# Splitting the first dense layer into three float32r products in a recommender kernel (AutoInt)

## Chip, cores and metric

One core of one Trainium2 chip runs the whole kernel. The time is the device time of one execution in microseconds (us), as the median of several runs. TensorE is called PE below, VectorE DVE, ScalarE ACT, GpSimd POOL and the queue of SyncE SP.

## The reference

```python
offsets = jnp.arange(NUM_FIELDS, dtype=X.dtype) * VOCAB_PER_FIELD
embed_x = emb_table[X + offsets[None, :]]          # 2048 x 39 x 64
att = embed_x
for i in range(LAYERS):                            # 3
    att = _mhsa(att, WQ[i], WK[i], WV[i], WR[i])   # 2 heads, softmax over 39 fields, + x @ Wr, relu
att_output = jax.nn.relu(att.reshape(B, FLAT) @ Wlin)
h = embed_x.reshape(B, FLAT)                       # 2048 x 2496
h = jax.nn.relu(h @ W1 + b1)                       # 512 wide: the layer that changes
h = jax.nn.relu(h @ W2 + b2)                       # 256 wide
dnn_output = jax.nn.relu(h @ W3 + b3)
return jax.nn.sigmoid(att_output + dnn_output)
```

All inputs are float32.

## The kernel before

The batch of 2048 is cut into 16 tiles of 128 samples. A tile has 24 units: 3 attention layers of 8 units, each unit 16 samples. One step of the main loop handles one unit at several stages, so a tile takes 24 steps (numbered `ts` 0 to 23) and the kernel 384 steps and a few more. Every engine runs a program of its own, in the order that is written out by hand; only semaphores order the engines against each other.

In step s PE does, in this order: two split products into the banks X0 and X1 (three float32r matmuls each: low part times high weight, high part times low weight, high times high), one piece of the dense branch (`dense`), a transpose of one chunk of embeddings (`embedding`, in 20 of the 24 steps), a third split product into Ob, eight transposes of the softmax of unit s-2, the scores of unit s (32 matmul records, into the bank SV) and the attention of unit s-2 (into Ob). The scores wait until ACT has copied the values of the unit before out of SV (`v_ready`).

The dense branch of a tile is spread over its steps. The first dense layer has FC = 20 chunks of 128 rows of W1 (the last has 64) and `first_layer` does one of them in each step ts = 0 to 18 and 23: embT[chunk] as weights (128 x 128), w1[chunk] as moving operand (128 x 512), into bank Mb. Both are float32. A float32 matmul stands in the trace as two records. The steps 19 to 22 hold the transposes of h1 and the second layer.

ACT does in a step: relu of Ob into xs (layers 0 and 1), copy of the transposed embedding chunk into embT, x_hi (a rounding of xs to float32r), two copies yv, the exponential, the copy v_sb and the two copies pt. DVE does: two maxima mx, two subtractions sd, in 8 of 24 steps the weighted output `prod`, x_lo = xs - x_hi, in 8 steps the sum over `prod` (`summed`, at ts = SUM_AT onwards), and, once ACT has written the exponential, den, rd and pn. POOL issues the gathers of embedding rows and shuffles embT into xs for the next tile.

Ahead of the loop, the weights come in on SP's queue (W1 in one transfer of 4,864 KB and one of 128 KB), PE and DVE make the split attention weights (`weights_ready`), and PE, ACT and DVE transpose, copy and shuffle the first tile in NB = 5 blocks of 4 chunks. POOL may run 20 gathers ahead and goes on as blocks are transposed.

Of the kernel before, what the change touches and what calls it, by code (L numbers as in the profile page):

```python
# [14 lines left out]
def autoint(nc, X, table, WQ, WK, WV, WR, W1, b1, W2, b2, W3, b3, Wlin, out):  # L15
# [42 lines left out]
    L2_AT = H1T_AT + 1  # L58
    L2_LAST = L2_AT + len(L2_PARTS) - 1

    SUM_AT = 4
# [45 lines left out]
    with ctx:  # L107
# [13 lines left out]
        w1 = sb("w1", [128, FC, N1])  # L121
# [13 lines left out]
        xs = sb("xs", [128, L, XC])  # L135
        prod = sb("prod", [128, UL, C])
# [8 lines left out]
        pe_sb = sb("pe_sb", [KR, G, H, F])  # L145
# [31 lines left out]
        weights_ready = sem("weights_ready")  # L177
        idx_ready = sem("idx_ready")
# [42 lines left out]
        LD_D = 16 * 7  # L221
# [15 lines left out]
        def layer_of(u):  # L237
            return (u % NU) // UL
# [11 lines left out]

        def layer_cols(u):

            return slice((u % UL) * C, (u % UL + 1) * C)

        def x_pair(u, e, p):
            at = (u % UL) * C + p * F
            return xs[64 * e:64 * e + D, layer_of(u), at:at + F]
# [6 lines left out]
        def _(sp):  # L264
# [9 lines left out]
            for e in range(2):  # L274
                sp.dma_start(wl_in[:, e, :], Wlin.rearrange("(f d) o -> f (d o)", f=F)).then_inc(ld_w, 16)
            sp.dma_start(w1[:, 0:FC - 1, :],
                         W1[0:(FC - 1) * 128, :].rearrange("(c p) n -> p c n", p=128)).then_inc(ld_d, 16)
            sp.dma_start(w1[0:LASTW, FC - 1, :], W1[(FC - 1) * 128:, :]).then_inc(ld_d, 16)
# [4 lines left out]
            sp.dma_start(b3_b[:], b3[None, :].to_broadcast([128, 1])).then_inc(ld_d, 16)  # L283

# [71 lines left out]
        def _(pe):  # L356
# [111 lines left out]
            pe.wait_ge(first_embT, NB)  # L468
            first_layer(0, 0)
# [42 lines left out]
        def _(act):  # L512
# [13 lines left out]
            def split_high(u):  # L526
# [6 lines left out]
                nc.scalar.copy(x_hi[:, u % XS, :], xs[:, layer_of(u), layer_cols(u)]).then_inc(xh_ready, 1)  # L533

            act.wait_ge(weights_ready, 1)
            for k in range(NB):
                first_embedding(k)
            for u in range(LEAD):
                split_high(u)
            for s in range(STEPS):  # L540
                t, ts = tile_step(s)
                u = s - NEW_AT
                if 0 <= u < TOTAL and layer_of(u) < L - 1:
                    act.wait_ge(o_ps, u + 1)
                    nc.scalar.activation(xs[:, layer_of(u) + 1, layer_cols(u)], Ob[:, 0:C], ACTF.Relu).then_inc(x_new, 1)  # L545
# [22 lines left out]
                if 0 <= u < TOTAL:  # L568
                    at_least(act, o_ps, u)
                    for j in range(2):  # L570
                        act.wait_ge(t_ps, 2 * u + j + 1)
                        nc.scalar.copy(pt[:, j * (G // 2):(j + 1) * (G // 2), :, :].rearrange("q g b f -> q (g b) f"),  # L572
                                       XB[j][0:KR, :].rearrange("q (n f) -> q n f", f=64)[:, :, 0:F]).then_inc(pt_ready, 1)
            act.wait_ge(fin_pe, 2)
# [136 lines left out]
```

## Time and profile before

| | |
|---|---|
| median of 3 runs | 2049.63 us (2048.24 to 2055.91) |
| the profiled execution | 2049.93 us, span 2048.0 us |
| PE busy | 95% of the span |
| DVE, ACT, POOL busy | 79%, 63%, 42% |
| share of PE in the chain that ended last | 94% |
| mean granted TensorE clock | 0.994 |

The profile shows one execution. Its span is the time from the first instruction to the last; the rest of its 2049.93 us lies around it. Matmuls are pipelined, so their recorded durations overlap; how far apart their ends are tells what one costs. The chain of waits gives just that, as the time that each piece adds.

### The profile page before, as it was taken

To read this page: it belongs to the slowest core of one execution; us is meant where nothing else is said; L and a number is where in the kernel's file an instruction comes from. 1 tells how busy PE (TensorE), PEld (TensorE's weight loads), DVE (VectorE), ACT (ScalarE), POOL (GpSimd) and SP (SyncE) were. 2 spreads that over 40 slices of the span, in tenths; PEclk is the share of its full clock that TensorE was granted. 3 is DMA by queue.
4 is the path that set the end of the run, shared out by engine and by line. 5 is a ranking of instruction groups with operands and counts; after the bars stand their busy time and mean duration, and the time that the engine had idled before them with its cause. 6 is when DMAs were issued, how large, how long until landed. Compare 5 with 4: busy or idle time off the path is not lost.

```text
span 2048.0 us, 103306 instructions
## 1 busy us (share of the span) xinstructions
PE 1954.7 (95%) x44640; PEld 1612.0 (79%) x44640; DVE 1614.2 (79%) x3429; ACT 1289.5 (63%) x3269; POOL 860.0 (42%) x949
## 2 busy tenths in 40 slices
PE   1598999999999999999999999999999999999998
PEld 0377888887888888888888888888888888887887
DVE  2376778887787888878788787888888788887887
ACT  0265666666666666666666666666666666666665
POOL 6544354444444444454444434444443444443000
PEclk9999999999999999999999999999999999999999
DMA  4111111111111111111111111111111111111000
GB/s 151 23 28 25 31 27 32 29 30 31 27 33 27 31 29 30 31 29 31 29 30 29 28 33 27 32 29 30 31 27 33 27 32 28 30 30 26 21 19 17
DMA packets 67561, 64.61 MB, mean 32 GB/s; under 512 B 23768, under 2 KB 54504, under 8 KB 67112
## 3 DMA queue, kind: packets, MB, share of 16 engines
q1 hardware_dynamic: 47144, 37.52, 6.2%
q0 software_dynamic: 19968, 20.49, 5.1%
q8 instruction: 357, 5.85, 1.2%
q14 instruction: 92, 0.75, 0.1%
HBM read 27.24 MB, written 0.01 MB: 13 GB/s over the span
## 4 chain that ended last, share of the span: by engine, by line
PE 94%; another core or an unknown queue 2%; issue 1%; DVE 1%; POOL 1%; SPq 1%; ACT 0%; DMA 0%; ACTq 0%
PE SV L445 21%; PE Ob L462 14%; PE Mb L400 13%; PE X L430 13%; PE X L423 9%; PE X L425 5%; PE X L424 5%; PE Ob L423 3%; PE Ob L424 3%; PE Ob L425 3%; PE Ob L391 2%; PE Mb L416 1%; POOL emb L324 1%; PE Mb L411 0%
## 5 line engine op out<-in xcount | busy, mean ns | idle before, releaser
L324 POOL DMA_INDIRECT emb<-L_rec_emb_table,idx_t x624 | 630.1, 1010 | 792.4 <-PE Ob L462 615.1
L666 DVE TENSOR_REDUCE den<-pe_sb 103x16 f32<-103x624 f32 x384 | 308.5, 803 | 316.3 <-ACT pe_sb L561 311.5
L445 PE MATMUL SV<-yv,xs 64*39 64x142 f32 x12288 | 455.0, 286 | 11.6 <-ACT v_sb L563 10.9
L445 PEld LDWEIGHTS SV<-yv,xs 64*39 64x39 f32 x12288 | 345.2, 113 | 53.0 <-issue 14.1
L545 ACT ACTIVATE xs<-Ob 128x312 f32<-128x312 f32 x256 | 110.6, 432 | 388.2 <-PE Ob L462 388.2
L648 DVE TENSOR_REDUCE mx<-SV 103x8 f32<-103x312 f32 x768 | 332.7, 474 | 26.9 <-PE SV L445 20.4
L462 PEld LDWEIGHTS Ob<-pt,v_sb 39*32 39x32 f32 x12288 | 273.2, 106 | 92.8 <-issue 91.8
L430 PE MATMUL X<-ident,pn 103*103 103x103 f32 x3072 | 341.8, 254 | 0.0
L572 ACT COPY pt<-X 103x312 f32<-103x312 f32 x768 | 284.8, 424 | 78.6 <-PE X L430 39.1
L400 PE MATMUL Mb<-w,embT 128*128 128x512 f32 (+1 forms) x640 | 331.7, 599 | 0.9 <-ACT embT L518 0.7
L462 PE MATMUL Ob<-pt,v_sb 39*32 39x39 f32 x12288 | 324.1, 198 | 7.8 <-issue 6.6
L653 DVE TENSOR_TENSOR sd<-SV,mx 103x312 f32<-103x312 f32 x768 | 330.5, 471 | 0.1
L430 PEld LDWEIGHTS X<-ident,pn 103*103 103x103 f32 x3072 | 329.7, 170 | 0.0
L671 DVE TENSOR_TENSOR pn<-pe_sb,rd 103x624 f32<-103x624 f32 x384 | 311.7, 812 | 13.3
L555 ACT COPY yv<-X 128x312 f32<-128x312 f32 x768 | 297.7, 433 | 35.9 <-PE X L425 17.7
L462 PE MATMUL Ob<-pt,v_x 39*32 39x39 f32 x12288 | 313.1, 198 | 3.5 <-issue 2.7
L301 POOL COPY xs<-embT 64x256 f32<-64x256 f32 x300 | 222.7, 742 | 214.9 <-ACT embT L524 78.9
L561 ACT ACTIVATE pe_sb<-sd 103x624 f32<-103x624 f32 x384 | 284.3, 740 | 2.2 <-DVE sd L653 2.1
L423 PE MATMUL X<-x_lo,w_hi 128*128 128x312 f32 x768 | 276.5, 360 | 2.8 <-DVE x_lo L607 2.0
L462 PEld LDWEIGHTS Ob<-pt,v_x 39*32 39x32 f32 x12288 | 262.7, 106 | 3.9 <-issue 3.1
L425 PE MATMUL X<-x_hi,w_hi 128*128 128x312 f32 x768 | 236.1, 307 | 1.7 <-issue 1.7
L424 PE MATMUL X<-x_hi,w_lo 128*128 128x312 f32 x768 | 236.1, 307 | 1.2 <-issue 1.2
(71 smaller groups left out, 2336.6 us busy)
## 6 DMA issues: line engine op xcount, KB each, us to landing
v_x<-v_sb SPq DMA_DIRECT2D x768, 39.0 KB
emb<-L_rec_emb_table,idx_t POOLq DMA_INDIRECT x624
w<-L_rec_W SPq DMA_DIRECT2D x1, 4864.0 KB
w<-L_rec_W SPq DMA_DIRECT2D x1, 512.0 KB
idx_in<-r_X SPq DMA_DIRECT2D x1, 312.0 KB, 3.9
b_b<-L_rec_b SPq DMA_DIRECT2D x1, 256.0 KB
w<-L_rec_W SPq DMA_DIRECT2D x1, 128.0 KB
b_b<-L_rec_b SPq DMA_DIRECT2D x1, 128.0 KB
```

Of the source, the lines that this page charges most:

```text
L324: nc.gpsimd.indirect_dma_start(out=emb[:, n % ER, f % 2 * D:(f % 2 + 1) * D], out_offset=None, in_=table, in_offset=bass.IndirectOffsetOnA ...
L400: return nc.tensor.matmul(Mb[:], embT[0:w, t % 2, n, :], w1[0:w, n, :], start=(n == 0), stop=(n == FC - 1))
L423: nc.tensor.matmul(out_ps, w_hi[:, l, at:at + 128], x_lo[:, slot, :], start=True, stop=False)
L424: nc.tensor.matmul(out_ps, w_lo[:, l, at:at + 128], x_hi[:, slot, :], start=False, stop=False)
L425: return nc.tensor.matmul(out_ps, w_hi[:, l, at:at + 128], x_hi[:, slot, :], start=False, stop=True)
L430: last = nc.tensor.transpose(XB[j][0:KR, g * 128:g * 128 + KR], pn[:, u % PS, j * (G // 2) + g, :, :].rearrange("q h f -> q (h f)")[:, 0:K ...
L445: last = nc.tensor.matmul(SV[64 * b:64 * b + F, at:at + YR], x_pair(u, e, p), yv[64 * e:64 * e + D, l, p, :], start=True, stop=True, skip_ ...
L462: last = nc.tensor.matmul(Ob[po:po + DH, p * F:(p + 1) * F], v, pt[lo:lo + F, g, b, :], start=False, stop=True, skip_group_check=True)
L648: nc.vector.tensor_reduce(mx[:, regions(j), :], sv_scores[:, regions(j)], AX.X, ALU.max).then_inc(mx_ready, 1)
L653: nc.vector.tensor_tensor(sd[:, gs], sv_scores[:, gs], mx[:, gs, :, None].to_broadcast([KR, G // 2, H, F]), ALU.subtract).then_inc(sd_read ...
L666: nc.vector.tensor_reduce(den[:], pe_sb[:], AX.X, ALU.add).then_inc(den_ready, 1)
L671: nc.vector.tensor_tensor(pn[:, s % PS, :, :, 0:F], pe_sb[:], rd[:, :, :, None].to_broadcast([KR, G, H, F]), ALU.mult).then_inc(pn_ready, 1)
```

## The change

W1 is no longer kept in float32. It comes in chunk by chunk through four slots, which lie in the second buffer of xs; ACT rounds each chunk into w1_hi and DVE writes the remainder w1_lo, both float32r. In the loop ACT rounds a chunk of embT into c_hi at the end of a step (`convert_high`), and DVE writes c_lo = embT - c_hi right behind x_lo (`convert_low`), for the chunk that PE uses two steps later. PE then does three float32r matmuls of 512 columns in place of one float32 matmul. To make room, the inputs of layers 1 and 2 share one buffer of xs, the weighted outputs go there too, and the exponential is written over sd. `summed` begins at ts = 0 and no longer at ts = 4.

```diff
+    CONVERT_AHEAD = 2
+    CR = 3
+    WS = 4
-    SUM_AT = 4
+    SUM_AT = 0
...
-        w1 = sb("w1", [128, FC, N1])
+        w1_hi = sb("w1_hi", [128, FC, N1], F32R)
+        w1_lo = sb("w1_lo", [128, FC, N1], F32R)
...
-        xs = sb("xs", [128, L, XC])
-        prod = sb("prod", [128, UL, C])
+        c_hi = sb("c_hi", [128, CR, TB], F32R)
+        c_lo = sb("c_lo", [128, CR, TB], F32R)
+        xs = sb("xs", [128, 2, XC])
+        w1_in = xs[:, 1, 0:WS * N1].rearrange("q (s n) -> q s n", n=N1)
...
-        pe_sb = sb("pe_sb", [KR, G, H, F])
+        pe_sb = sd
...
+        def converted_at(s):
+            t, n = tile_step(s + CONVERT_AHEAD + 1)
+            return (t, n) if n < FC and t < TILES else None
...
+            for n in range(FC):
+                w = LASTW if n == FC - 1 else 128
+                at_least(sp, w1_lo_ready, n - WS + 1)
+                sp.dma_start(w1_in[0:w, n % WS, :], W1[n * 128:n * 128 + w, :]).then_inc(ld_w1[n % WS], 16)
...
             def first_layer(t, n):
-                w = LASTW if n == FC - 1 else 128
-                if t > 0:
-                    pe.wait_ge(embT_ready, chunk_count(t, n))
+                i = t * FC + n
+                pe.wait_ge(c_lo_ready, i + 1)
                 if n == 0:
                     at_least(pe, h2_ready, t)
-                return nc.tensor.matmul(Mb[:], embT[0:w, t % 2, n, :], w1[0:w, n, :], start=(n == 0), stop=(n == FC - 1))
+                nc.tensor.matmul(Mb[:], c_lo[:, i % CR, :], w1_hi[:, n, :], start=(n == 0), stop=False)
+                nc.tensor.matmul(Mb[:], c_hi[:, i % CR, :], w1_lo[:, n, :], start=False, stop=False)
+                return nc.tensor.matmul(Mb[:], c_hi[:, i % CR, :], w1_hi[:, n, :], start=False, stop=(n == FC - 1))
...
+            pe.wait_ge(w1_lo_ready, FC)
             first_layer(0, 0)
...
+            def convert_high(t, n):
+                i = t * FC + n
+                w = LASTW if n == FC - 1 else 128
+                chunk_embedded(act, t, n)
+                if i >= CR:
+                    at_least(act, o_ps, (i - CR) // FC * NU + (i - CR) % FC - PV_AT)
+                    act.wait_ge(c_lo_ready, i - CR + 1)
+                nc.scalar.copy(c_hi[0:w, i % CR, :], embT[0:w, t % 2, n, :]).then_inc(c_hi_ready, 1)
...
             for k in range(NB):
+                for n in range(k * BK, (k + 1) * BK):
+                    w = LASTW if n == FC - 1 else 128
+                    act.wait_ge(ld_w1[n % WS], 16 * (n // WS + 1))
+                    nc.scalar.copy(w1_hi[0:w, n, :], w1_in[0:w, n % WS, :]).then_inc(w1_hi_ready, 1)
                 first_embedding(k)
...
+                    if layer_of(u) == 0:
+                        at_least(act, lin_sum, (u // NU - 1) * UL + u % UL + 1)
...
+            def convert_low(t, n):
+                i = t * FC + n
+                w = LASTW if n == FC - 1 else 128
+                dve.wait_ge(c_hi_ready, i + 1)
+                nc.vector.tensor_tensor(c_lo[0:w, i % CR, :], embT[0:w, t % 2, n, :], c_hi[0:w, i % CR, :],
+                                        ALU.subtract).then_inc(c_lo_ready, 1)
```

On ACT, a step of the loop of the second tile, with an output of layer 0 or 1 and an embedding chunk, reads before:

```order
L533 CAST x_hi<-xs 128x312 [waits o_ps,x_new]
L555 COPY yv<-X 128x8x39 [waits y_ps,sv_ps]
L555 COPY yv<-X 128x8x39 [waits y_ps]
L561 ACTIVATE pe_sb<-sd 103x624 [waits sd_ready,pn_ready]
L563 COPY v_sb<-SV 103x512 [waits o_ps]
L572 COPY pt<-X 103x312 [waits t_ps,o_ps]
L572 COPY pt<-X 103x312 [waits t_ps]
L545 ACTIVATE xs<-Ob 128x312 [waits o_ps]
```

and in the changed kernel:

```order
L566 CAST x_hi<-xs 128x312 [waits o_ps,x_new]
L607 COPY yv<-X 128x8x39 [waits y_ps,sv_ps]
L607 COPY yv<-X 128x8x39 [waits y_ps]
L613 ACTIVATE sd<-sd 103x624 [waits sd_ready,pn_ready]
L615 COPY v_sb<-SV 103x512 [waits o_ps]
L624 COPY pt<-X 103x312 [waits t_ps,o_ps]
L624 COPY pt<-X 103x312 [waits t_ps]
L576 CAST c_hi<-embT 128x128 [waits c_lo_ready,o_ps,embT_ready]
L597 ACTIVATE xs<-Ob 128x312 [waits lin_sum,o_ps]
```

The new instruction c_hi stands between the copies pt and the relu of the next step; nothing else has moved.

On DVE, the step ts = 1 of the second tile, which is the fullest one of the changed kernel, reads before:

```order
L648 TENSOR_REDUCE mx<-SV 103x8 [waits sv_ps] x2
L653 TENSOR_TENSOR sd<-SV,mx 103x312 [waits mx_ready,e_ready]
L653 TENSOR_TENSOR sd<-SV,mx 103x312 [waits mx_ready]
L624 SCALAR_TENSOR_TENSOR prod<-Ob,wl 128x312 [waits embT_ready,o_ps]
L607 TENSOR_TENSOR x_lo<-xs,x_hi 128x312 [waits xh_ready]
L666 TENSOR_REDUCE den<-pe_sb 103x16 [waits e_ready]
```

and in the changed kernel:

```order
L719 TENSOR_REDUCE mx<-SV 103x8 [waits sv_ps] x2
L724 TENSOR_TENSOR sd<-SV,mx 103x312 [waits mx_ready,e_ready]
L724 TENSOR_TENSOR sd<-SV,mx 103x312 [waits mx_ready]
L695 SCALAR_TENSOR_TENSOR xs<-Ob,wl 128x312 [waits embT_ready,o_ps]
L663 TENSOR_TENSOR x_lo<-xs,x_hi 128x312 [waits xh_ready]
L671 TENSOR_TENSOR c_lo<-embT,c_hi 128x128 [waits c_hi_ready]
L704 TENSOR_REDUCE red<-xs 128x8 [waits lin_mult]
L739 TENSOR_REDUCE den<-sd 103x16 [waits e_ready]
```

Two instructions have come in between x_lo and den: c_lo, and the sum that stood four steps later before.

## Rows read from the trace of the kernel before

**Rows 1.** The page: span, busy time, TensorE's clock in 40 slices

```profile
span 2048.0 us, 103306 instructions
PE 1954.7 (95%) x44640; PEld 1612.0 (79%) x44640; DVE 1614.2 (79%) x3429; ACT 1289.5 (63%) x3269; POOL 860.0 (42%) x949
PEclk9999999999999999999999999999999999999999
```

**Rows 2.** Chain of waits, one step: start us, us added, what

```profile
1002.88 0.34 PE X L423
1003.23 0.14 PE X L424
...
1003.94 0.86 PE Mb L400 x2
...
1004.91 0.14 PE Ob L423
...
1007.99 0.34 PE X L423
```

**Rows 3.** Groups by line and shape: busy us, mean ns

```profile
L400 PE MATMUL Mb<-w,embT 128*128 128x512 f32 x608 | 312.8, 595 | 0.9 <-ACT embT L518 0.7 <-issue 0.2
L424 PE MATMUL X<-x_hi,w_lo 128*128 128x312 f32 x768 | 236.1, 307 | 1.2 <-issue 1.2
```

**Rows 4.** Timeline of that step: ACT, then PE's scores

```profile
1002.94 0.43 ACT L545 ACTIVATE xs<-Ob 128x312 f32<-128x312 f32 x1 [1.42 <-PE Ob L462]
1003.27 0.26 ACT L524 COPY embT<-Ob 128x128 f32<-128x128 f32 x1
1003.41 0.47 ACT L533 CAST x_hi<-xs 128x312 fp32r<-128x312 f32 x1
...
1005.01 0.61 ACT L563 COPY v_sb<-SV 103x512 f32<-103x512 f32 x1
...
1006.00 1.18 PE L445 MATMUL SV<-yv,xs 64*39 64x142 f32 x32
```

**Rows 5.** Timeline of DVE: that step's den, then a step ts = 22

```profile
1005.18 0.80 DVE L666 TENSOR_REDUCE den<-pe_sb 103x16 f32<-103x624 f32 x1 [0.86 <-ACT pe_sb L561]
...
1061.86 0.42 DVE L678 TENSOR_TENSOR h<-Mb,b_b 128x256 f32<-128x256 f32 x1
1062.19 0.86 DVE L648 TENSOR_REDUCE mx<-SV 103x8 f32<-103x312 f32 x2
...
1063.75 0.47 DVE L624 SCALAR_TENSOR_TENSOR prod<-Ob,wl 128x312 f32<-128x312 f32 x1
1064.14 0.47 DVE L607 TENSOR_TENSOR x_lo<-xs,x_hi 128x312 fp32r<-128x312 f32 x1
1064.76 0.80 DVE L666 TENSOR_REDUCE den<-pe_sb 103x16 f32<-103x624 f32 x1 [0.15 <-ACT pe_sb L561]
...
1066.61 0.47 DVE L648 TENSOR_REDUCE mx<-SV 103x8 f32<-103x312 f32 x1
```

**Rows 6.** Chain of waits ahead of the loop

```profile
15.73 18.92 another core or an unknown queue
...
38.77 1.13 PE Mb L382 x4
...
40.16 0.95 POOL emb L324
...
63.07 2.25 DMA emb<-L_rec_emb_table,idx_t
...
65.58 0.44 PE Mb L382
...
72.26 13.01 another core or an unknown queue
```

**Rows 7.** Stretches: busy us of PE, PEld, DVE, ACT, POOL, PEclk, DMA share, GB/s

```profile
20.00:25.00 5.00, 0.00 (x0) 0.00 (x0) 0.00 (x0) 0.00 (x0) 3.78 (x4) 1.00 1.06 396
30.00:35.00 5.00, 0.00 (x0) 0.00 (x0) 0.33 (x2) 0.00 (x0) 0.94 (x1) 1.00 0.43 135
```

More of the change, by code:

```diff
@@ L177, in autoint @@
         weights_ready = sem("weights_ready")
+        ld_w1 = [sem(f"ld_w1_{k}") for k in range(WS)]
+        w1_hi_ready = sem("w1_hi_ready")
+        w1_lo_ready = sem("w1_lo_ready")
+        c_hi_ready = sem("c_hi_ready")
+        c_lo_ready = sem("c_lo_ready")
         idx_ready = sem("idx_ready")
@@ L249, in last_outputs, with x_buffer, weighted_outputs, chunk_embedded @@
             return u // NU * UL + max(u % NU + 1 - (NU - UL), 0)
+        def x_buffer(l):
+            return min(l, 1)
+        def weighted_outputs(u):
+            return xs[:, 1, layer_cols(u)].rearrange("q (p f) -> q p f", f=F)
+        def converted_at(s):
+            t, n = tile_step(s + CONVERT_AHEAD + 1)
+            return (t, n) if n < FC and t < TILES else None
+        def chunk_embedded(eng, t, n):
+            if t > 0:
+                eng.wait_ge(embT_ready, chunk_count(t, n))
+            else:
+                eng.wait_ge(first_embT, n // BK + 1)
         def layer_cols(u):
@@ L532, in split_high @@
                 at_least(act, o_ps, u - XS + 1)
-                nc.scalar.copy(x_hi[:, u % XS, :], xs[:, layer_of(u), layer_cols(u)]).then_inc(xh_ready, 1)
+                nc.scalar.copy(x_hi[:, u % XS, :], xs[:, x_buffer(layer_of(u)), layer_cols(u)]).then_inc(xh_ready, 1)
+            def convert_high(t, n):
[6 more added lines that the diff above has]
+                nc.scalar.copy(c_hi[0:w, i % CR, :], embT[0:w, t % 2, n, :]).then_inc(c_hi_ready, 1)
             act.wait_ge(weights_ready, 1)
             for k in range(NB):
+                for n in range(k * BK, (k + 1) * BK):
+                    w = LASTW if n == FC - 1 else 128
+                    act.wait_ge(ld_w1[n % WS], 16 * (n // WS + 1))
+                    nc.scalar.copy(w1_hi[0:w, n, :], w1_in[0:w, n % WS, :]).then_inc(w1_hi_ready, 1)
                 first_embedding(k)
+                if k == 0:
+                    for n in range(CONVERT_AHEAD + 1):
+                        convert_high(0, n)
             for u in range(LEAD):
@@ L606, in split_low @@
                 dve.wait_ge(xh_ready, u + 1)
-                nc.vector.tensor_tensor(x_lo[:, u % XS, :], xs[:, layer_of(u), layer_cols(u)], x_hi[:, u % XS, :],
+                nc.vector.tensor_tensor(x_lo[:, u % XS, :], xs[:, x_buffer(layer_of(u)), layer_cols(u)], x_hi[:, u % XS, :],
                                         ALU.subtract).then_inc(xl_ready, 1)
-            for k in range(NB):
+            def convert_low(t, n):
[4 more added lines that the diff above has]
+                                        ALU.subtract).then_inc(c_lo_ready, 1)
+            for k in range(NB):
+                for n in range(k * BK, (k + 1) * BK):
+                    w = LASTW if n == FC - 1 else 128
+                    dve.wait_ge(w1_hi_ready, n + 1)
+                    nc.vector.tensor_tensor(w1_lo[0:w, n, :], w1_in[0:w, n % WS, :], w1_hi[0:w, n, :],
+                                            ALU.subtract).then_inc(w1_lo_ready, 1)
                 dve.wait_ge(first_embT, k + 1)
+                if k == 0:
+                    for n in range(CONVERT_AHEAD + 1):
+                        convert_low(0, n)
                 for e in range(2):
@@ L622, in weighted @@
                     dve.wait_ge(embT_ready, chunk_count(*chunk_at(u + PV_AT)))
-                at_least(dve, lin_sum, last_outputs(u) - UL)
-                nc.vector.scalar_tensor_tensor(out=prod[:, u % UL, :].rearrange("q (p f) -> q p f", f=F),
+                nc.vector.scalar_tensor_tensor(out=weighted_outputs(u),
                                                in0=Ob[:, 0:C].rearrange("q (p f) -> q p f", f=F), scalar=0.0,
```

17 lines of the change are left out of this document (10 added, 7 removed).

## The prediction

> **What bounds the kernel now.** I read the page first: PE is busy 95% of the span, DVE 79%, ACT 63%, and TensorE's clock stands at full speed nearly throughout [rows 1]. A busy PE is not by itself the bound, since its records overlap, so I went to the chain of waits. In the loop it consists of PE alone: one step runs from 1002.88 to 1007.99 without another engine in it [rows 2], 5.11 us. What shortens PE's work therefore shortens the step, until another engine's work for one step is longer than what is left of PE's. So the next question is how far away those are.
>
> ACT: from the end of the attention it runs without a pause through relu, embT, x_hi, yv, the exponential and v_sb, and is done with v_sb at 1005.01 + 0.61 = 1005.62; PE starts the scores, which wait for v_sb, at 1006.00 [rows 4]. The slack is 0.38 us a step. The loop over ACT (attention, ACT's row of work, scores, attention) is thus 5.11 - 0.38 = 4.73 us. After the pt copies ACT idles 1.42 us until the attention ends [rows 4].
>
> DVE: it waits 0.86 us a step for the exponential in an ordinary step, and still 0.15 us at ts = 22 with its extra work [rows 5]. Its loop is bound by the exponential, so by ACT's place in PE's step, not by its own sum.
>
> **The change, part by part.** *PE, removed:* one float32 matmul of 512 columns, two records, adds 0.86 us to the chain [rows 2]; the group's mean of 595 ns a record [rows 3] counts overlap and is not the price. At full clock its 0.43 us a record are 2 clock cycles (of 2.4 GHz) for each of 512 columns.
>
> *PE, added:* three float32r matmuls of 512 columns. The trace has none of that width, but it has the same kind at 312 columns: 0.14 us each in the chain [rows 2], which at 2.4 GHz is one cycle a column, 0.130 us, and some 0.01 us more. Upper bound by width: 0.14 x 512/312 = 0.236, three make 0.71. Lower bound with no extra at all: 512 columns at one cycle, 0.213, three make 0.64. If the extra 0.014 (the pieces alternate between 0.14 and 0.15) stays as it is for an instruction, one costs 0.227 and three 0.68. I take 0.69, nearer the measured kind than the ideal. The saving is 0.17 us a chunk, between 0.15 and 0.22. There are 16 x 20 = 320 chunks, all of them on PE's path: 54 us, between 48 and 70.
>
> The Trainium skill (TensorE: Matmul & The Clock Gate, Back-to-back issue gap) gives N/2.4 + 2.5 ns for the gap between warm matmuls, which by estimate would be 216 ns here and a saving of 0.21 us a chunk, 68 us. For the 312 columns that rule says 132 ns; the rows have 0.14, so the trace lies a little above it, and the sum goes by the rows.
>
> *PE, waits:* the first of the three waits for c_lo. It is made two steps ahead, some 4 us before PE is there, and c_hi's wait for its old buffer is for a matmul of the step before. Nothing is queued late behind either.
>
> *ACT, added:* c_hi, 128 x 128. The copy of the same size into embT moves the next start by 0.14 us (1003.27 to 1003.41) [rows 4]. It stands where ACT idles 1.42 us; cost nothing. If that cover were gone it would add 0.14 to a loop of 4.73 = 4.87 us, and the new PE step is 5.11 - 0.17 = 4.94. Even then it stays hidden.
>
> *DVE, added:* c_lo, 128 x 128. The 256-column operation takes 0.33 us from start to next start (1061.86 to 1062.19), the 312-column x_lo is 0.47 us recorded and the prod ahead of it 0.39 from start to start (1063.75 to 1064.14) [rows 5]. Down to 128 columns that line gives 0.20. It lies inside the 0.86 us wait for the exponential. The fullest step is ts = 0 or 1, which now also has the sum: den to the next mx 1.85, mx and sd 1.56, prod 0.39, x_lo 0.39, c_lo 0.20, sum 0.39 (as prod) make 4.78 us [rows 5]. That is below 4.94, so it fits, with little to spare; if c_lo cost as much as x_lo, 0.39, it would be 4.97 and hold two steps of a tile by 0.03, 1 us in all. The earlier sum also meets the new wait of ACT on `lin_sum`: it is done three steps before that relu. Steps ts = 19 to 22 have no chunk and gain nothing. I take off 1 us for steps in which DVE or its prod holds PE.
>
> The exponential written over sd adds no wait: DVE reads it in its own order before it writes sd again. One shared buffer for the later layers: its columns are read by the scores of the same unit before relu writes them. Both at nothing.
>
> *Ahead of the loop:* Before, DVE sits from 15.73 for 18.92 us [rows 6], released by something that the profile doesn't name. In that time the DMA engines are full with W1 (share 1.06, 396 GB/s), and it ends 2 or 3 us after the transfers do [rows 7]. All that follows hangs on it: split attention weights, first transposes at 38.77, and POOL, out of its 20 slots, goes on with gathers only at 40.16 [rows 6], after some 9 us of idleness. Its last gather then starts at 63.07, lands 2.25 later, and the last transposes are at 65.58 [rows 6]. In the changed kernel only four chunks of W1 (1 MB) can be under way until the splits free slots. With 1.1 MB of other weights that is 2.1 MB at 390 GB/s, 5.5 us; if the stop is a matter of full DMA engines, DVE goes on at about 22, weights are ready at 26, POOL never stops, and the last transposes come 9 us earlier. The splits have to keep up: five blocks of four chunks, per block on DVE 4 x 0.6 (under twice the 256-column step) and four shuffles at 0.47, the recorded time of an operation of that size [rows 5], or the reload of the slots, by estimate a landing of 2 to 3 us as the gather's 2.25 [rows 6] and the splits behind it: 4 to 6 us a block; from 26 that ends near 55, before the last gather's 57. If the stop stays as it is, the splits run from 39 and end near 65, so nothing is lost nor won. A second such stop at 72.26 of 13.01 us [rows 6] I leave as it is. SP's queue now has 20 transfers with waits ahead of the first v_x, which is needed only after that second stop.
>
> **The sum**, against the profiled execution's 2049.93 us (the median of the runs is 2049.63, the same to 0.02%): 2049.9 - 54 + 1 - 9 = 1988 us. Without the 9 it is 1997.
>
> **The rivals.**
> (a) *The saving in the loop comes, the start stays as it is:* 1997 us. For it: a second stop of the same kind comes at 72.26, when the load of W1 is long over, so full DMA engines may not be the cause. Against it: the end of the first stop coincides with the end of W1.
> (b) *PE at the ideal rate:* a pass of 0.213 to 0.216 us gives 68 to 70 us, 1971 us with the 9. Against it: 0.14 for 312 columns.
> (c) *ACT or DVE takes over:* the step falls only to ACT's loop or DVE's sum. By the numbers above that starts under 4.78 us, so it costs at most a few us; if c_hi and c_lo were dearer, say 0.4 each, and DVE came to 5.0 in the 20 steps with a chunk, half of the saving would go: some 2015 us.
> (d) *Slower:* the price of a pass at 512 columns. It decides at 0.86/3 = 0.287 us a pass: above that the three passes are dearer than what they replace. If 512 float32r columns ran at the two cycles of the float32 record, 0.43, three would be 1.29, 0.43 more a chunk, 320 x 0.43 = +138 us: 2188 us. For it speaks only that no such width is in the trace, and that the first pass of a step stands at 0.34 [rows 2], which is the wait behind the attention; against it the 0.14 of five of six passes.
>
> **How the numbers follow.** Forecast (loop and start) 0.5; (a) 0.27; (b) 0.1; (c) 0.08; (d) and anything else that makes it slower 0.05. The likeliest is 1988 us. The range takes in the bounds of a pass (48 to 70 us), the start at 0 to 9 us and either of the two stops shorter or longer by a few us: 1971 to 2008 us. It leaves out (d) and most of (c). A difference of 0.5%, 10 us, is about what a measurement of this kernel can tell from none. Faster by more than that: 0.92; within it: 0.03; slower: 0.05.
>
> **What would show it.** Right: three pieces of 0.23 us in the chain where 0.86 stood, PE still alone in the chain, steps of about 4.94 us, v_sb ending 0.2 us before the scores; DVE's wait for the exponential near 0.6 us in an ordinary step; first transposes near 26 us and the loop's first scores some 9 us earlier. Wrong: a pass of 0.24 us or more; ACT or DVE named in the chain inside the loop; the stop at 15.73 as long as before; PE waiting for c_lo.

## The result, and the profile after

The changed kernel takes 2038.8 us (median of 5 runs, 2034.86 to 2039.32), the kernel before 2050.53 in the same session: ratio 0.9934, 95% interval 0.9918 to 0.995. It is faster, by 12 us (0.7%) where 62 were forecast, and outside the range of 1971 to 2008. The profiled executions have spans of 2048.0 before [rows 1] and 2032.9 after, 15 us apart; the one after is the fastest of its five runs. All runs of a kernel in a session agree within 1%, but for one of `h1_in_wait` with 4471 us, which no ratio counts.

The page of the kernel after, to be read against [rows 1], and two groups of it (busy us, mean ns of one, idle time ahead and what ended it):

```profile
span 2032.9 us, 105044 instructions
PE 1915.6 (94%) x44960; PEld 1680.0 (83%) x44960; DVE 1691.4 (83%) x3771; ACT 1353.2 (67%) x3609; POOL 892.0 (44%) x949
PE 86%; DVE 5%; issue 4%; ACT 3%; another core or an unknown queue 1%; POOL 1%; DMA 0%; ACTq 0%
L477 PE MATMUL SV<-yv,xs 64*39 64x142 f32 x12288 | 455.5, 285 | 19.1 <-ACT v_sb L615 11.1
L739 DVE TENSOR_REDUCE den<-sd 103x16 f32<-103x624 f32 x384 | 308.1, 802 | 230.4 <-ACT sd L613 210.3
```

PE's busy time fell by 39 us and its share hardly at all. The chain of waits of one step, where [rows 2] had 0.86 for the layer:

```profile
1084.85 0.34 PE X L455
...
1085.91 0.23 PE Mb L430
1086.14 0.23 PE Mb L431
1086.37 0.23 PE Mb L432
...
1087.94 1.18 PE SV L477 x32
```

Three passes take 0.69 to 0.71, in the mean 0.70; a chunk is cheaper by 0.16: this part came as priced. The same step on ACT, and PE's rows around it (timeline; start us, us), as [rows 4] for before:

```profile
1084.78 0.41 PE L455 MATMUL X<-x_lo,w_hi 128*128 128x312 f32 x1
1085.11 0.43 ACT L597 ACTIVATE xs<-Ob 128x312 f32<-128x312 f32 x1 [1.44 <-PE Ob L494]
1087.19 0.60 ACT L615 COPY v_sb<-SV 103x512 f32<-103x512 f32 x1
1087.94 1.18 PE L477 MATMUL SV<-yv,xs 64*39 64x142 f32 x32
1090.06 0.43 ACT L597 ACTIVATE xs<-Ob 128x312 f32<-128x312 f32 x1 [1.43 <-PE Ob L494]
```

From relu's start to v_sb's end ACT takes 1085.11 to 1087.79, 2.68 us, just as long as before (1002.94 to 1005.62 [rows 4]). But PE's scores now start 0.15 behind v_sb's end, where 0.38 lay before, and from the scores to the next relu it takes 2.12. The step is 4.95. That is 2.68 + 0.15 + 2.12, a closed loop over ACT and PE. So PE stands in the chain alone and yet seems to be held by ACT: the wait at v_sb is short, and the chain puts it into the scores, whose piece is 1.18 here and 1.11 in a step without the wait (as in most of the kernel before). Whether ACT really sets the step is what the first experiment asks.

To see where the rest is, I measured the length of each step, from its first row of scores to that of the next step, in the timelines of both kernels (tiles 2 to 15, counted from 1; the number of the step is that of its first scores; medians, and for the tile the mean; "17+18" are two steps together, and the last column says when the scores of the whole kernel's second step start):

```
                         ts 4-8   ts 9   ts 11   17+18   tile    second scores at
before                   5.05     5.47   5.07    10.07   121.3   88.4
after                    4.96     6.22   4.97    10.25   120.6   84.8
```

Of 3.2 us a tile that PE gave back (20 chunks of 0.16) 0.7 arrived. The step at ts = 9 is 0.75 longer; it already stood out before, by 0.4. Its rows, tile 9, POOL, PE and DVE:

```profile
1107.15 0.96 POOL L355 DMA_INDIRECT emb<-L_rec_emb_table,idx_t  x1 [0.27 <-POOL xs L332]
1108.42 1.54 POOL L355 DMA_INDIRECT emb<-L_rec_emb_table,idx_t  x1 [0.30 <-issue]
1107.80 1.18 PE L477 MATMUL SV<-yv,xs 64*39 64x142 f32 x32
1109.54 0.19 PE L494 MATMUL Ob<-pt,v_x 39*32 39x39 f32 x1 [0.34 <-issue]
1110.30 0.27 PE L494 MATMUL Ob<-pt,v_sb 39*32 39x39 f32 x3 [0.47 <-issue]
1110.33 0.87 DVE L719 TENSOR_REDUCE mx<-SV 103x8 f32<-103x312 f32 x2 [1.19 <-PE SV L477]
```

In the middle of the attention PE stops twice, with no semaphore that the profile shows, and DVE gets the end of the scores 1.19 us late; both go on at the same moment, 1110.3. POOL's second gather runs from 1108.42 to 1109.96, beside the end of the scores and most of both stops. And two steps of a tile, 17 and 18, gained nothing (10.07, 10.25): there the weighted output (`xs<-Ob,wl`, L695) is late on DVE, and PE's product into Ob waits for it (a row of the groups):

```profile
L455 PE MATMUL Ob<-x_lo,w_hi 128*128 128x312 f32 x384 | 148.9, 388 | 9.5 <-DVE xs L695 9.5
```

Ahead of the loop, DVE's rows at the two stops of [rows 6], and POOL's last gather of the first burst:

```profile
31.28 0.35 DVE L650 COPY embT<-Ob 64x192 f32<-64x192 f32 x1 [15.50 <-remote]
30.63 0.94 POOL L355 DMA_INDIRECT emb<-L_rec_emb_table,idx_t  x1 [0.30 <-issue]
78.91 0.48 DVE L719 TENSOR_REDUCE mx<-SV 103x8 f32<-103x312 f32 x1 [5.29 <-remote]
```

In the chain the second stop is 9.35 us (from 71.67), where [rows 6] had 13.01. The first stop is 15.5 us instead of 18.9, though the DMA engines are no longer full in it (windows of the kernel after, columns as in [rows 7]):

```profile
25.00:30.00 5.00, 0.00 (x0) 0.00 (x0) 0.00 (x0) 0.00 (x0) 3.78 (x5) 1.00 0.14 27
```

The second scores come 3.6 us earlier, not 9. Even that is not sure: in two more profiles of the changed kernel (`after_again`, `after_third`, below) they start at 86.7 and 90.4, on either side of the 88.4 of before. So there were four questions: what holds ordinary steps at 4.95, what stretches ts = 9, what holds 17 and 18, and what the stops are.

### The profile page after: what moved, and what is told of

It reads as the page before. It is cut to its first block, busy times and chain, and to the rows that moved or that the text cites. A ratio compares the mean times of both kernels' runs of the same rounds, so it can differ in the third digit from the quotient of the medians.

```text
span 2032.9 us, 105044 instructions
## 1 busy us (share of the span) xinstructions
PE 1915.6 (94%) x44960; PEld 1680.0 (83%) x44960; DVE 1691.4 (83%) x3771; ACT 1353.2 (67%) x3609; POOL 892.0 (44%) x949
## 4 chain that ended last, share of the span: by engine, by line
PE 86%; DVE 5%; issue 4%; ACT 3%; another core or an unknown queue 1%; POOL 1%; DMA 0%; ACTq 0%
PE SV L477 20%; PE Ob L494 14%; PE X L462 12%; PE X L455 8%; PE X L456 5%; PE X L457 5%; PE Mb L430 3%; PE Mb L432 3%; PE Mb L431 3%; PE Ob L455 3%; PE Ob L456 2%; PE Ob L457 2%; PE Ob L422 2%; PE Mb L448 1%
## 5 line engine op out<-in xcount | busy, mean ns | idle before, releaser
L355 POOL DMA_INDIRECT emb<-L_rec_emb_table,idx_t x624 | 648.6, 1039 | 758.9 <-PE Ob L494 567.2
L739 DVE TENSOR_REDUCE den<-sd 103x16 f32<-103x624 f32 x384 | 308.1, 802 | 230.4 <-ACT sd L613 210.3
L477 PEld LDWEIGHTS SV<-yv,xs 64*39 64x39 f32 x12288 | 349.8, 112 | 65.6 <-issue 38.0
L332 POOL COPY xs<-embT 64x256 f32<-64x256 f32 x300 | 236.2, 787 | 207.4 <-ACT embT L557 79.4
L744 DVE TENSOR_TENSOR pn<-sd,rd 103x624 f32<-103x624 f32 x384 | 311.9, 812 | 13.7 <-DVE rd L741 0.4
L624 ACT COPY pt<-X 103x312 f32<-103x312 f32 x768 | 294.4, 435 | 26.3 <-PE X L462 13.2
L613 ACT ACTIVATE sd<-sd 103x624 f32<-103x624 f32 x384 | 284.8, 742 | 4.3 <-DVE sd L724 3.9
L615 ACT COPY v_sb<-SV 103x512 f32<-103x512 f32 x384 | 227.7, 593 | 0.0
```

The costliest lines, as they stand in the source:

```text
L355: nc.gpsimd.indirect_dma_start(out=emb[:, n % ER, f % 2 * D:(f % 2 + 1) * D], out_offset=None, in_=table, in_offset=bass.IndirectOffsetOnA ...
L477: last = nc.tensor.matmul(SV[64 * b:64 * b + F, at:at + YR], x_pair(u, e, p), yv[64 * e:64 * e + D, l, p, :], start=True, stop=True, skip_ ...
L739: nc.vector.tensor_reduce(den[:], pe_sb[:], AX.X, ALU.add).then_inc(den_ready, 1)
L744: nc.vector.tensor_tensor(pn[:, s % PS, :, :, 0:F], pe_sb[:], rd[:, :, :, None].to_broadcast([KR, G, H, F]), ALU.mult).then_inc(pn_ready, 1)
```

## The experiments

The runs were made in sessions, on more than one chip. The kernel before is 35 us faster in two of them (2013 and 2017 us) than in the others (2048 to 2053), and in those two no trace has a stop ahead of the loop; "with stops" and "without" say which kind a session was. The chip as such need not be the reason: the record gives the same chip number, 2, to one session with stops (`after_third`) and to one without (`after_fourth`). Where the expectations below speak of a chip with or without stops, read session. Each kernel is compared with before in its own session; the changed kernel was run again in three of them. TensorE's granted clock is 0.99 with stops and 1.00 without, and the steps at ts 4 to 8 are equally long (4.96), so the clock is not what differs.

**Ordinary steps: ACT.** `one_pass` leaves two of the three passes out, so that it computes only c_hi x w1_hi of the first dense layer:

```diff
-                nc.tensor.matmul(Mb[:], c_lo[:, i % CR, :], w1_hi[:, n, :], start=(n == 0), stop=False)
-                nc.tensor.matmul(Mb[:], c_hi[:, i % CR, :], w1_lo[:, n, :], start=False, stop=False)
-                return nc.tensor.matmul(Mb[:], c_hi[:, i % CR, :], w1_hi[:, n, :], start=False, stop=(n == FC - 1))
+                return nc.tensor.matmul(Mb[:], c_hi[:, i % CR, :], w1_hi[:, n, :], start=(n == 0), stop=(n == FC - 1))
```

> Of the three passes of the first dense layer only c_hi x w1_hi is left; the two small products are left out. It takes 2 x 0.23 us off PE in 320 steps. Theory (ACT and DVE set the ordinary steps with three passes already): steps with a chunk go from 4.95 to no less than 4.85 us, 5 to 30 us in all, and PE waits for v_sb in each. Rival (PE sets the step): 4.50 us, 148 us less.

1990.01 us (2 runs), ratio to before 0.9883 (0.9865 to 0.9901), without stops, where the changed kernel has 0.9884. By the chain's price PE lost 147 us of work (640 passes of 0.23), and the kernel nothing that can be measured. Its steps at ts 4 to 8 are 4.96; PE's row for the scores, and the one after it:

```profile
1059.36 1.18 PE L475 MATMUL SV<-yv,xs 64*39 64x142 f32 x32 [0.47 <-ACT v_sb L613]
1061.49 0.43 ACT L595 ACTIVATE xs<-Ob 128x312 f32<-128x312 f32 x1 [1.44 <-PE Ob L492]
```

PE now waits 0.47 us for v_sb, and the loop over ACT is the same to 0.01: about 4.95 is a floor, and the changed kernel's ordinary steps stand on it. The steps at ts 0 and 1 do not: they fell from 4.90 to 4.77.

`xhi_early` was to shorten ACT's row by moving x_hi ahead of relu:

```diff
+                if s + LEAD < TOTAL:
+                    split_high(s + LEAD)
                 u = s - NEW_AT
                 if 0 <= u < TOTAL and layer_of(u) < L - 1:
...
-                if s + LEAD < TOTAL:
-                    split_high(s + LEAD)
```

> ACT makes x_hi of two steps ahead before it waits for the end of the attention, instead of behind relu and embT; nothing else is changed. Theory (ACT's and DVE's row of work sets the ordinary step of the changed kernel: relu, embT, x_hi, yv, exponential, v_sb end 0.14 us before the scores, and that is only the wake-up): x_hi's 0.14 us leaves the row, ordinary steps fall from 4.95 to about 4.86 us, and the kernel by 320 x 0.06 to 0.09, 15 to 25 us. Rival (PE alone still sets the step, and 0.70 us for three passes is all there is): steps stay at 4.95 and the time within 4 us.

2039.77 us, 0.9949 (0.9937 to 0.9962): nothing won. The experiment did not do what it was for. With five slots x_hi waits for the end of the same attention as relu, so the row begins with x_hi instead and is no shorter; steps at ts 4 to 8 are 5.01. It showed one thing: x_hi, which reads no PSUM (the matrix accumulators' memory), starts as late behind the scores (2.19) as relu does in the changed kernel (2.14), so relu does not start late because it reads PSUM. A sixth slot, with which x_hi would not have to wait (`xhi_early6`, expected 4.70 to 4.86 a step), needs more on-chip memory than there is, so that experiment has no result.

`v_first` takes the exponential out of the loop instead of x_hi:

```diff
-                    nc.scalar.activation(pe_sb[:], sd[:], ACTF.Exp).then_inc(e_ready, 1)
                     at_least(act, o_ps, u - VS + 1)
                     nc.scalar.copy(v_sb[:, u % VS, :, :, :], sv_values).then_inc(v_ready, 1)
+                    nc.scalar.activation(pe_sb[:], sd[:], ACTF.Exp).then_inc(e_ready, 1)
```

> On ACT the copy of v_sb comes ahead of the exponential instead of behind it; both still wait for DVE's sd. Theory (ACT's row from the attention to v_sb sets the ordinary steps at 4.95): v_sb is there 0.6 us earlier, PE no longer waits for it, steps fall to PE's own 4.86 to 4.91, 8 to 15 us less than the changed kernel. Rival (DVE, whose next maxima wait behind the exponential, den and pn): the exponential is 0.47 us later, DVE goes over 4.95, and the kernel is 5 to 60 us slower.

2027.54 us, 0.9888 (0.9865 to 0.9911); the changed kernel beside it (`after_again`) 2036.1, 0.9924 (0.9897 to 0.995). Both theories saw something: with the exponential behind the copy, steps at ts 4 to 8 fell from 4.96 to 4.86, and those in which DVE has extra work rose, 17 and 18 from 10.25 to 10.64, 19 to 23 from 24.33 to 25.02 together. So there are two loops over ACT, one through v_sb and PE and one through the exponential and DVE, and which is the longer depends on the step. But the total says less than it seems: the step at ts = 9 fell too, from 6.20 to 5.12, some 16 us in all, which is more than the whole gain of 9. By this sum the order on ACT alone would have lost. `v_first_part` has the new order at ts = 2 to 16 alone (`early = 2 <= ts <= 16`, and the exponential on either side of the copy by it).

> v_sb ahead of the exponential only at ts = 2 to 16; in the other steps the order of the changed kernel. With it in all steps the ordinary ones fell from 4.95 to 4.85 us, and those with extra work on DVE rose (ts = 18 from 5.3 to 5.85, 20 from 4.69 to 5.02, 22 from 5.02 to 5.34). Theory (two loops: through v_sb on ACT and through the exponential on DVE): both are served, 1.2 us a tile more than with v_sb first everywhere, 18 to 25 us less than the changed kernel. Rival (DVE's lateness is carried from one step to the next): the steps behind ts = 16 stay long, no better than 8 us.

2012.88 us, 0.98 (0.978 to 0.982), against 2039.52, 0.9935, of the changed kernel beside it: 26.6 us. Its row on ACT and PE's scores:

```profile
1087.81 0.43 ACT L597 ACTIVATE xs<-Ob 128x312 f32<-128x312 f32 x1 [0.95 <-PE Ob L494]
1089.64 0.59 ACT L617 COPY v_sb<-SV 103x512 f32<-103x512 f32 x1 [0.24 <-issue]
1090.72 1.18 PE L477 MATMUL SV<-yv,xs 64*39 64x142 f32 x32
```

v_sb ends 0.49 ahead of the scores; step and tile are 4.87 and 118.3 (120.3 beside it). The lateness of DVE is not carried on: 19 to 23 are 24.34 again. Of the 2.0 us a tile, however, 0.87 (mean of tiles 2 to 15) lie in the step at ts = 9, where POOL's gathers shifted against PE. That is some 13 us of the 26.6; the order on ACT itself brought the rest, 14 to 17 us.

**ts = 9: the gathers.** Four kernels. `before_late_gather` puts `nc.gpsimd.memset(pad[:], 0.0)` ahead of the gathers of ts = 9 in the kernel before, `gather_in_time` has `FIELDS_AT` with 0, 3 in place of 1, 2 at ts = 8 and 9, `gather_ring11` the same with `ER = 11` for 10.

> The kernel before the change, with a filling of an unused 128 x 512 buffer on POOL (some 0.5 us) ahead of the gathers of ts = 9. Theory (the time of POOL's gather against the scores sets the stretch): the second gather moves from 0.07 to about 0.6 us behind the start of the scores, and the step goes from 5.5 us to 6.0 to 6.2, 8 to 11 us in all. Rival (the stretch comes from the changed kernel's own work): no change, within 3 us.

> In each tile POOL issues no gather at ts = 8, ahead of its four shuffles, and three at ts = 9 in place of two. Theory (a gather that POOL issues while PE is in scores and attention holds PE up; at ts = 9 POOL is late, its second gather runs 0.6 to 2.2 us behind the start of the scores and the attention ends at 3.05 instead of 1.71): POOL is no longer late at ts = 9, its third gather only touches the start of the scores, that step falls from 6.2 or more to 5.0 to 5.3 us, 0.9 to 1.3 us a tile, 13 to 20 us in all. Rival (the stretched step belongs to something that happens in PE's own program at ts = 9): it stays at 6.2 us and the time within 3 us.

> As the kernel with no gather at ts = 8 and three at ts = 9, but with 11 slots for the gathered rows instead of 10. With 10 POOL stood 2.34 us at ts = 9 until PE's transposes had freed a slot, and its third gather ran 0.95 to 2.17 us behind the start of the scores. Theory (only a gather beside scores and attention costs): the gathers of ts = 9 end ahead of the scores, that step is 4.95 to 5.1 us, 1.2 to 1.5 us a tile under the changed kernel, 18 to 23 us in all. Rival (three gathers in one step cost PE as much wherever they lie): the step stays at 5.5.

All three missed. before_late_gather: 2018.51 us, 1.0021 (1.001 to 1.0031), the step 5.42, where 6.0 was expected; gather_in_time: 1995.31, 0.9911 (0.9895 to 0.9926), the step 5.48; gather_ring11: 2032.74, 0.9926 (0.9907 to 0.9945), the step 6.14. Two things were wrong in them. Three gathers don't fit: POOL starts its first one some 0.8 to 1.0 us behind the end of the attention, so that in gather_in_time and gather_ring11 the third lay 0.95 to 2.2 us behind the start of the scores. And the price depends on the session: the changed kernel has the same gathers at the same places in either kind, and its step is 6.22 with stops and 5.39 without (`after_fourth`). The first two ran without stops, where there was little to see; there gather_in_time is no better than the changed kernel (0.9911 against 0.9884).

`second_waits` holds only the second gather back:

```diff
-                for f in fields_at(s)[1]:
+                for i, f in enumerate(fields_at(s)[1]):
+                    if ts == 9 and i == 1:
+                        at_least(pool, o_ps, s - PV_AT + 1)
                     gather(fields_at(s)[0], f)
```

> At ts = 9 POOL's second gather waits until the attention of that step is over, so that it can't run beside it; nothing else is changed. Three gathers in that step did not fit between attention and scores (POOL starts them 0.7 to 0.9 us behind the end of the attention), so the step stayed at 6.17 with them. Theory (the gather beside scores and attention is what stretches the step at ts = 9): it falls from 6.2 to 4.95 to 5.05 us, no other step rises, 1.1 us a tile, 15 to 18 us less than the changed kernel on a chip like the first, 5 to 9 on one like the second. Rival (the stretch is PE's own at ts = 9): it stays.

2038.27 us, 0.9923 (0.9902 to 0.9943), beside 2039.52 of the changed kernel. The step at ts = 9 is 4.98 instead of 6.20, and that at ts = 11 6.19 instead of 4.97. POOL at ts = 11, and PE's chain there:

```profile
1118.02 0.97 POOL L355 DMA_INDIRECT emb<-L_rec_emb_table,idx_t  x1 [0.27 <-POOL xs L332]
1119.30 1.54 POOL L355 DMA_INDIRECT emb<-L_rec_emb_table,idx_t  x1 [0.30 <-issue]
```

```profile
1118.68 1.18 PE SV L479 x32
1119.86 0.26 PE Ob L496 x10
1120.11 0.32 issue
1120.43 0.28 PE Ob L496 x3
1120.71 0.49 issue
1121.19 0.73 PE Ob L496 x49
```

It is the picture of ts = 9, stop for stop, in another step: scores at 1118.68, the second gather 0.62 behind them (0.62 at ts = 9 of the changed kernel, 1107.80 and 1108.42). The stretch belongs to the gather, not to PE's program. It only moved, probably since the waiting made POOL late: its first gather of ts = 11 begins 0.7 us ahead of the scores instead of 2.2. Nothing was won in all.

v_first_part shows the same inside one trace, at ts = 9. In nine of its tiles 2 to 15 the second gather ends at most 0.62 us behind the start of the scores, and the step is 4.85 to 5.21; in the other five it runs from some 0.6 to some 1.55 behind it, and the step is 5.79 to 5.89. With 0.6 to 2.16, in the changed kernel, it is 6.2. In two tiles of the changed kernel it runs from 1.3 to 2.3, and the step is 8.35 and 8.39. So the later the gather lies against the scores, the longer the step, with one tile of the changed kernel that doesn't fit (0.47 to 1.42, 6.18).

**Steps 17 and 18.** `h1_in_wait` moves DVE's h1 addition behind x_lo of the next step:

```diff
+                if ts == H1T_AT - 1:
+                    dve.wait_ge(l1_ps, t + 1)
+                    nc.vector.tensor_tensor(h1[:], Mb[:], b1_b[:], ALU.add).then_inc(h1_ready, 1)
                 if converted_at(s):
                     convert_low(*converted_at(s))
...
-                if ts == H1T_AT - 2:
-                    dve.wait_ge(l1_ps, t + 1)
-                    nc.vector.tensor_tensor(h1[:], Mb[:], b1_b[:], ALU.add).then_inc(h1_ready, 1)
```

> DVE's h1 addition (0.6 us) moves from the end of ts = 17 to behind x_lo of ts = 18, where DVE waits for the exponential. Theory (at ts = 17 and 18 the changed kernel is held by DVE: weighted is late, and PE's product for Ob waits for it): these two steps shorten by 0.3 to 0.8 us a tile, 5 to 12 us in all. Rival (PE's transposes of h1 or another engine hold these steps anyway): the time stays within 3 us, or grows since the h1 transposes wait for the later addition.

2049.44 us, 1.0001 (0.999 to 1.0012): worse than the changed kernel by some 10 us (in another session). The rival was right: PE's transposes of h1 then wait for the addition, and the two steps are 11.03. That the addition makes DVE late stays argued from the order of its rows; a way to take it away was not found.

**The stops.** `gather_after_weights` has `pool.wait_ge(weights_ready, 1)` ahead of POOL's first gather:

> POOL issues its first gather only once the attention weights are split, instead of at 6 us. Theory (the stop from 15.78 to 31.25 is the same thing as the one at 71.67: PE's signal waits for the end of POOL's burst): the stop shrinks to under 1 us, and the split weights are there near 20 us instead of 35; the gathers then end later, near 68 us instead of 62, so the first scores come up to 6 us later. Rival (the stop belongs to the start of the program or to the loads): it stays at some 15 us with no gather running, and everything moves by 29 us.

2049.56 us, one run. Its DVE at the place of the first stop, and its chain at that of the second:

```profile
14.71 1.08 DVE L646 COPY yv<-embT 128x512 f32<-128x512 f32 x3
15.83 0.35 DVE L651 COPY embT<-Ob 64x192 f32<-64x192 f32 x1
...
18.51 1.36 DVE L658 TENSOR_TENSOR w_lo<-embT,w_hi 128x1152 fp32r<-128x1152 f32 x1
```

```profile
76.59 18.60 another core or an unknown queue
```

```profile
90.19 0.95 POOL L355 DMA_INDIRECT emb<-L_rec_emb_table,idx_t  x1 [0.30 <-issue]
```

No gather, no stop: DVE goes on at once, and the split weights are there 15 us earlier. In exchange one burst of all gathers runs up to the second stop, which is 18.6 us and ends 4 us behind the last gather at 91.14. `gather_ring11`, with two gathers more in the first burst (to 33.5 instead of 31.6), had a first stop of 21.6 us; but as the unedited kernel had 15.5, 17.2 and 19.0 us in three profiles, that alone says little. Nor does a stop end just with its burst: DVE goes on 0.3 us ahead of the end of the last gather in the profile above (31.28 and 31.57), and 3.6 us behind it in after_third. And `spread_first`, with `FIRST_FIELDS_AT = 5 * [3] + 12 * [2]`:

> The first tile's steps ask for 3 gathers in each of five steps and then 2, instead of 10 in the first step. Theory (the stop of 9.35 us at 71.67 comes from POOL's unbroken burst of gathers, during which what PE signals from the scores arrives late): the burst behind the first scores has 3 gathers in place of 10, the stop shrinks to under 3 us, 6 to 9 us less in all. Rival (the stop belongs to PE's program or to the first scores as such): it stays at 9 us and the time within 3 us.

2029.53 us, 0.9916 (0.99 to 0.9931). The second stop on DVE is 3.85 us instead of 5.29, but gather_ring11, whose gathers are not spread, has 3.81 as well. The second scores start at 81.4 us. In the two other kernels with spread gathers and stops (combo and best, below) it is 79.1 and 80.6; in nine traces with stops and the old burst, after, after_again and after_third among them, it is 82.4 to 90.9. So some us are won ahead of the loop, not how many; in the total the changed kernel has 0.9924 to 0.9935 in other sessions, and the intervals overlap.

The same rows where there are no stops, in `after_fourth`, the changed kernel unedited:

```profile
16.94 0.94 POOL L355 DMA_INDIRECT emb<-L_rec_emb_table,idx_t  x1 [0.30 <-issue]
16.19 0.35 DVE L650 COPY embT<-Ob 64x192 f32<-64x192 f32 x1
```

POOL issues the same burst and DVE doesn't stop. In another session without stops before_late_gather, which is the kernel before up to the loop, has this window, with W1 on its way, just where the stop would be:

```profile
16.00:18.00 2.00, 0.00 (x0) 0.00 (x0) 1.95 (x5) 0.00 (x0) 1.52 (x2) 1.00 0.96 348
```

DVE is busy through it, and the last split of the attention weights starts at 18.48. DMA engines full of W1 are thus neither needed for a stop to go on nor enough to make one.

**The same kernel in both kinds of session, and edits together.**

> The changed kernel once more, unedited, on the chip of the next three. The kernel before runs 35 us faster on a second chip than on the first one, and there its trace has neither stop ahead of the loop. Theory (the small gain is made of losses inside the loop, the same on every chip: ordinary steps held at 4.95, the step at ts = 9 stretched to 6.2, nothing won at ts = 17 and 18): 10 to 18 us less than before on either kind of chip. Rival (the loss belongs to the stops at the start, which came out badly in the changed kernel): where there are no stops the gain is near the 54 us of the passes.

> The changed kernel unedited, as the measure for the three that follow, since chips differ by some 35 us ahead of the loop. If they run on a chip like the first: 12 to 15 us less than before. If on one without the stops: theory (the losses lie in the loop) 8 to 18 us less than before; rival (they lie in the stops) some 50.

> The changed kernel unedited, as the measure for the two that follow: 11 to 15 us less than before on a chip with the stops; on one without them 8 to 18 us less if the losses lie in the loop, some 50 if they lie in the stops.

The changed kernel: 2036.1 us, 0.9924; 2039.52, 0.9935 (0.9917 to 0.9953); and without stops 1992.14, 0.9884 (0.9865 to 0.9903), 24.5 us less than before. The loss in the loop is there in both kinds; it is larger with stops, by about what the step at ts = 9 costs more (0.83 us a tile, 12 us).

> Three edits of the changed kernel together: v_sb ahead of the exponential, no gather at ts = 8 with three at ts = 9 and 11 slots, and 3 gathers a step at the start instead of 10 in the first. If the three causes are separate their gains add: 25 to 40 us less than the changed kernel on a chip without the stops, some 6 more on one with them. If the exponential is held up by its new place, less than the two gather edits alone.

> The second gather of ts = 9 behind the attention, v_sb ahead of the exponential at ts = 2 to 16, and 3 gathers a step at the start instead of 10 in the first. If the causes are separate the gains add: 35 to 45 us less than the changed kernel on a chip like the first, 22 to 30 on one without stops.

combo: 2030.82 us, 0.9909 (0.9887 to 0.9931), no better than v_first alone. best: 2014.85, 0.981 (0.9791 to 0.9829), the same as v_first_part alone. In each the pair of gathers had moved beside the scores again (ts = 9 at 5.87, ts = 11 at 5.80), so what the start gave was lost there (and, in best, in the first tile, 141.8 us from the second scores to those of the next tile against 136.8 in v_first_part). The gains don't add while a stretch can move.

> v_sb ahead of the exponential at ts = 2 to 16 (26 us off the changed kernel), and 3 gathers a step at the start instead of 10 in the first. Theory (the second stop lasts as long as the burst of gathers behind the first scores, and has nothing to do with the loop): 6 to 8 us less than with v_sb alone, 32 to 35 us under the changed kernel, on a chip with the stops; nothing more on one without. Rival (what is won at the start is lost later, since the gathers are then behind): no better than 27 us under the changed kernel.

> As v_part_spread, and at ts = 9, 11, 13 and 14 POOL's second gather waits for the end of that step's attention. With the wait at ts = 9 alone the stretch moved to ts = 11 (from 4.91 to 6.17 us), where the same pair of gathers then lay beside scores and attention. Theory (the stretch goes where the gather goes): no step from 9 to 16 is over 5.0, 0.4 to 0.5 us a tile less than v_part_spread, 6 to 8 us in all. Rival (POOL's lateness grows and its shuffles hold the scores of the next tile, or it stretches a later step): the same as v_part_spread or slower.

Both without stops: 1970.4 us, 0.9768 (0.9754 to 0.9782), and 1969.86, 0.9766 (0.9752 to 0.978). That is 21.7 us under the changed kernel and 46 under before. Here the step at ts = 9 is 4.95 without any wait: with the other order on ACT the second gather ends 0.5 to 1.65 us behind the start of the scores, and no longer at 2.16. The four further waits gave nothing. In a session with stops v_part_spread was not run.

## Why the prediction was wrong

*PE's price of a pass: right.* 0.69 a chunk was forecast, 0.70 measured. Rival (b) is out, and so is (d). By the rule of the Trainium skill (TensorE: Matmul & The Clock Gate, Back-to-back issue gap) a chunk would by estimate be 0.65; the chain has 0.23 a pass, not 0.216.

*"The loop over ACT is thus 5.11 - 0.38 = 4.73 us": this step failed.* It took the whole distance between v_sb's end and the scores for slack, and the rest of the loop for fixed. In the medians of ts 4 to 8 the loop before is 5.05 - 0.39 = 4.66. Of the 0.39, 0.14 are the bare way from one engine to the other, and stay. And where PE has waited for v_sb, relu starts 2.14 behind the scores instead of 1.98 (0.30 behind PE's next start instead of 0.11). That makes 4.66 + 0.14 + 0.16 = 4.96, where PE's own step would have been 4.86 to 4.9. That the forecast of 4.94 a step came so near is luck: it started from 5.11, one step that stood for all, and took off the full saving. The floor took about 0.07 in each of some 12 steps a tile, 0.8 us, 13 in all. "ACT or DVE takes over", rival (c), was the right mechanism and had too small a chance, as it was tied to dearer copies. Its time of 2015 us was misreckoned besides: 5.0 us in place of 4.94 in 320 steps is 19 us, 2007 us and inside the range. c_lo costs what was said, 0.20 between starts; of c_hi, 0.14 was said, and three in a row ahead of the loop stand 0.20 apart. Both are hidden: c_hi ends long before relu starts. The sign that was named for this rival, ACT or DVE in the chain inside the loop, did not show it; PE stood there alone.

*DVE: half right.* The fullest ordinary step fits. The pair 17 and 18, with h1, the weighted output and the product that waits for it, was not looked at; it costs the 0.16 it should have gained and 0.18 more, 5 us in all.

*POOL's gathers were missing from the sum.* With shorter steps POOL's second gather of ts = 9 runs 0.62 to 2.16 us behind the start of the scores; in the kernel before it ran from 0.07 to 1.02. That made 0.75 us a tile, and the chunk's 0.16 there did not show: 13 to 14 us. With ACT's floor it is the largest loss, and no term or rival named it: this is the second step that failed. In the session without stops the step is 5.39, no longer than the 5.42 of before_late_gather, and the saving is larger, 24.5 us, but still under half of the 53 forecast for the loop; there the floor and the pair 17 and 18 are the losses that were found.

*The start: "if the stop is a matter of full DMA engines" was false.* The 9 us were 3.6 in the first pair of profiles, and nothing that can be told from the stops' own scatter (84.8, 86.7 and 90.4 after, 88.4 before). The doubt in rival (a), that the second stop comes when W1 is long loaded, was the right one.

The sum for the two profiled executions: forecast 62, found 15 (12 between the medians). 5 us at the start, 13 on ACT's floor, 14 at ts = 9, 5 at 17 and 18 make 37. 4 more are in the first tile, which took 132.0 us from the second scores on before and 132.9 after, instead of 3.2 less. Some 6 us are spread over steps at ts = 0 to 3, 22 and 23 (attention 0.77 instead of 0.72) and single long steps, and were not told apart.

## What to carry to other kernels

The distance between one engine's end and the other's start is not all slack; take from it what a bare wake-up costs in the same trace, and add up each loop through the other engines before a saving on the bounding one is believed. Then try the cheapest proof there is: leave the work out altogether, as one_pass did, and see whether anything moves. When a loop runs over a copy that is needed now and an operation that is needed later, look at the order of the two on their engine: with a swap in 15 of 24 steps 14 to 17 us came here, against 12 from the change of PE's arithmetic.

When steps get shorter, everything that is issued beside them at its own pace is somewhere else. Look for the busiest such engine, and see what its work then lies beside.

## What the runs showed of the hardware

In the sessions with stops, gathers that POOL issues hold up PE and what PE signals, if they lie beside the matmuls on parts of the array (the split weights at the start, scores and attention). A gather from 0.6 to 2.16 us behind the start of the scores makes the step 6.2 us instead of 4.95, one from 0.6 to 1.55 makes it 5.8 instead of 4.86 (v_first_part), and one that ends by 0.6 costs 0.35 or less. A burst of 20 or more makes DVE wait 15 to 21 us for matmuls that were over. A gather beside the products, transposes and dense layer did nothing that could be seen: at ts = 4 two of them run from 2.4 to 4.6 us behind the scores, and the step is 4.97. In the other sessions the same program has no stops, and the gather to 2.16 makes the step 5.39, 0.4 more instead of 1.25. What differs between the sessions, and by which way a gather reaches PE, stays open.

Relu starts 0.11 us behind PE's next start in steps where PE had not waited for v_sb, and 0.30 where it had (0.36 for x_hi in xhi_early). Why, the profile doesn't show; it makes the loop some 0.16 us longer just when it is the bound.
